# Layer 0 opens with image 0 in SBUF, evacuations on ScalarE, three eighths of v's first convolution on TensorE

## What is computed

```python
z   = group_norm(x)                       # 32 groups of 6 channels, per image
qkv = einsum('bchw,oc->bohw', z, w_qkv) + b_qkv
qkv = depthwise_conv3x3(qkv, w_dw) + b_dw # padding 1, 576 channels
q, k, v = split(qkv)                      # 4 heads of 48 channels, 4096 positions
q, k = l2norm(q), l2norm(k)
attn = softmax(q^T k * temperature)       # 4096 x 4096 per head
out  = einsum('oc,bchw->bohw', w_proj, attn v) + b_proj
x    = x + out
```

## Time and profile before

| what | value |
|---|---|
| median of 3 runs | 3560.64 us (3558.88 to 3561.38) |
| the profiled execution's own time | 3561.09 us |
| its span | 3559.3 us |
| TensorE (PE) busy | 3188.6 us, 90% |
| VectorE (DVE) busy | 1988.1 us, 56% |
| ScalarE (ACT) busy | 2096.1 us, 59% |
| GpSimd (POOL) busy | 1019.1 us, 29% |

### The profile page before, as it was taken

How to read it: one execution, slowest core, us unless ns; L and a number is a source line. 1 busy time by engine, 2 the same in 40 slices (tenths; PEclk the granted TensorE clock), 3 DMA queues, 4 the chain that set the end, 5 groups by cost and what they waited for, 6 DMA issues and landing times. The chain is left out here.

```text
span 3559.3 us, 48038 instructions
## 1 busy us (share of the span) xinstructions
PE 3188.6 (90%) x16424; PEld 1279.7 (36%) x16424; DVE 1988.1 (56%) x2522; ACT 2096.1 (59%) x2306; POOL 1019.1 (29%) x510
## 2 busy tenths in 40 slices
PE   1239999999999999999999966899999858999998
PEld 0012232222322323223222222455555424555555
DVE  4655243752257432563420145688888555888886
ACT  0015655556556565564666612688888415888886
POOL 1210202102021020020200003366566432666565
PEclk9669999999999999999999988999999979999999
DMA  6131212212103111131110033477777724877777
GB/s 179 45 77 28 60 42 45 57 45 55 50 24 77 44 37 50 35 78 32 25 44 7 10 90 92 102 139 146 145 143 139 159 75 99 145 138 144 145 144 132
DMA packets 691175, 295.71 MB, mean 83 GB/s; under 512 B 603314, under 2 KB 645042, under 8 KB 689266
## 3 DMA queue, kind: packets, MB, share of 16 engines
q1 hardware_dynamic: 690996, 293.45, 38.7%
HBM read 95.46 MB, written 34.28 MB: 36 GB/s over the span
## 5 line engine op out<-in xcount | busy, mean ns | idle before, releaser
L440 ACT ACTIVATE prob<-ps_s,cur 128x1024 f32<-128x1024 f32 x1024 | 1084.5, 1110 | 738.4 <-PE ps_s L514 736.8
L527 PE MATMUL ps_a<-prob,vt 128*64 128x512 f32 x4096 | 997.2, 608 | 0.0
L1132 POOL TENSOR_TENSOR p_lo<-gp,p_hi 128x1024 f16<-128x1024 f32 x256 | 551.9, 2166 | 402.9 <-ACT p_hi L1231 397.8
L1359 PE MATMUL ps_s<-kst,qs 128*128 128x512 f16 x2560 | 639.2, 383 | 20.3 <-DMA qs<-q_scratch 12.1
L1372 PE MATMUL ps_o<-v_hl,at_hi 128*128 128x384 f16 x2048 | 546.8, 328 | 28.4 <-DMA at_lo<-p_lo 26.9
L508 PE MATMUL ps_s<-q_a,k_a 128*128 128x512 f16 x2048 | 535.1, 383 | 7.6 <-issue 2.6
L1372 PE MATMUL ps_o<-v_hl,at_lo 128*128 128x192 f16 x2048 | 504.6, 247 | 0.0
L1606 DVE TENSOR_SCALAR_CACHE_REDUCE neg<-ps_s,mix 128x1024 f32<-128x1024 f32 x256 | 327.2, 1278 | 131.7 <-PE ps_s L1359 130.4
L527 PEld LDWEIGHTS ps_a<-prob,vt 128*64 128x64 f32 x4096 | 249.4, 136 | 412.4 <-issue 410.3
L1359 PEld LDWEIGHTS ps_s<-kst,qs 128*128 128x128 f16 x2560 | 244.8, 99 | 247.0 <-issue 23.3
L508 PEld LDWEIGHTS ps_s<-q_a,k_a 128*128 128x128 f16 x2048 | 138.0, 97 | 517.1 <-ACT prob L440 437.2
(11 more groups left out here) (176 smaller groups left out, 2763.2 us busy)
## 6 DMA issues: line engine op xcount, KB each, us to landing
z<-z_scratch SPq DMA_DIRECT2D x96, 384.0 KB, 3.9
sq<-rn_scratch SPq DMA_DIRECT2D x16, 768.0 KB, 10.6
qs<-q_scratch SPq DMA_DIRECT2D x64, 128.0 KB, 2.8
gn_x<-in_x SPq DMA_DIRECT2D x4, 1536.0 KB, 18.7
z_scratch<-gn_x SPq DMA_DIRECT2D x4, 1536.0 KB, 11.6
q_a<-hi SPq DMA_DIRECT2D x64, 96.0 KB, 2.4
rden<-den_scratch SPq DMA_DIRECT2D x64, 96.0 KB, 2.2
o_scratch<-o_s SPq DMA_DIRECT2D x64, 96.0 KB, 1.9
```

Source lines behind the costliest of these rows:

```text
L440: act.activation(prob[:, a % PR, :], ps_s[:, a % 2, :], ACT.Exp, bias=cur[:, slot:slot + 1], scale=1.0 / SPLIT).then_inc(exped, 1)
L527: ins = pe.matmul(ps_a[h * HALF:(h + 1) * HALF, j % 2, :], vt[:, slot, m, :], prob[:, a % PR, h * CH:(h + 1) * CH], start=(m == 0), stop=( ...
L1132: pool.tensor_tensor(p_lo[:, cols], prob[s][:, cols], p_hi[:, cols], ALU.subtract).then_inc(lo_made[c], 1)
L1359: ins = pe.matmul(ps_s[:, c % 2, h * CH:(h + 1) * CH], qs[:, s, qt, :], kst[:, ktile, cols], start=(t == 0), stop=(t == len(terms) - 1))
```

## The change

The block for the group norm is gone. In the new opening of layer 0:

- **Image 0 stays in SBUF.** It is loaded in four pieces of 96 x 2048, its statistics taken on VectorE (16 `bn_stats`, two more small links for a shift), and normalized there: channels 0 to 95 on VectorE, 96 to 191 on ScalarE, two halves of the pixels each. The first two projections read it in place (`project_first`); the store to `z_scratch` happens beside that.
- **Image 1's norm goes to ScalarE and GpSimd**, between other work: two copies and two squares of 96 x 4096 with an accumulated sum, two group sums on TensorE, five small GpSimd operations, two normalizing activations of 96 x 4096, all in ScalarE's program order.
- **Evacuations, squares, sums and `hi` of the first head go to ScalarE; `lo` of the first head to VectorE.** ScalarE's order holds image 1's normalization between v's third and fourth evacuated chunk.
- **The first convolutions run half by half** (`conv_half`): each tap waits for the tap before it. v's can start when five chunks are in `pad`.
- **Three eighths of v's first convolution** (chunks 5, 6, 7 of eight) become 27 products on TensorE with diagonal matrices `diag`, which ScalarE makes from `ident`; ScalarE evacuates them (`evac_far`). VectorE's second half shrinks to the 512 pixels of chunk 4.
- **The norm's root** of the first head comes from ScalarE's Sqrt and VectorE's reciprocal in place of GpSimd's power. The norm's factors come back in four pieces, each with its own semaphore. `load_z` of slot 2 now stands behind `split_out` in SP's order, followed by a wait for the last `evac_far`.
- **In the main loop** one thing changes: `split` forms u with one instruction of 112 rows in place of two of 48.

```diff
+                for c in range(4):
+                    cols = slice(c * NB, (c + 1) * NB)
+                    for h in range(2):
+                        sp.dma_start(sq[h * HALF:h * HALF + HD, cols],
+                                     rn_dram[h:h + 1, cols].partition_broadcast(HD)).then_inc(rn_first[c], 16)
+                sp.wait_ge(z_out, 16 * 2 * CT + 16 * CT)
+                sp.wait_ge(help_full, 18)
                 split_out(0, 0, None)
+                load_z(range(4), 2, 0, None)
+                sp.wait_ge(far_out, 8 - FAR)
...
             def _(act):
+                act.wait_ge(gn_op, 10)
+                for h in range(2):
+                    cols = slice(h * N // 2, (h + 1) * N // 2)
+                    act.activation(xin[:, 1, cols], xin[:, 1, cols], ACT.Identity,
+                                   bias=shift[:, 1:2], scale=gy[:, 1:2]).then_inc(z_high, 1)
+                for c in range(8):
+                    evac_project(0, c, 0)
+                for tap in range(TAPS):
+                    act.activation(diag[:, tap, :], ident[0:KR, 0:KR], ACT.Copy,
+                                   scale=vec[0:KR, 1, 1 + tap:2 + tap]).then_inc(diag_set, 1)
+                for t in range(CT):
+                    act.activation(vv[0:CP, :], xin[:, CT + t, :], ACT.Copy,
+                                   accum_out=total1[:, t:t + 1]).then_inc(gn1_op, 1)
...
+                for t in range(CT):
+                    act.activation(vv[0:CP, :], xin[:, CT + t, :], ACT.Square, bias=away1[:, t:t + 1],
+                                   accum_out=total1[:, t:t + 1]).then_inc(gn1_op, 1)
...
+                square(0)
+                square(1)
+                evac_sums(0)
+                for c in range(3):
+                    evac_project(1, c, 9)
+                act.wait_ge(gn1_pow, 5)
...
+                for t in range(CT):
+                    act.activation(xin[:, CT + t, :], xin[:, CT + t, :], ACT.Identity,
+                                   bias=shift1[:, t:t + 1], scale=gy1[:, t:t + 1]).then_inc(z1_made, 1)
+                evac_project(1, 3, CONV_OPS)
+                square(2)
+                evac_project(1, 4, CONV_OPS)
+                square(3)
+                evac_sums(1)
+                for c in range(5, 8):
+                    evac_project(1, c, CONV_OPS)
+                act.wait_ge(norm_asked, 1)
+                act.activation(nry[:, :, :], nrm[:, :, :], ACT.Sqrt).then_inc(powed, 1)
+                evac_far(5)
+                high(0)
+                high(1)
+                evac_far(6)
+                high(2)
+                high(3)
+                evac_far(7)
                 head(0, 0)
...
             def _(pe):
+                for c in range(FAR, 8):
+                    at = c - FAR
+                    for tap in range(TAPS):
+                        dy, dx = tap // 3, tap % 3
+                        ins = pe.matmul(ps_s[0:KR, at // 2, at % 2 * CH:(at % 2 + 1) * CH], diag[:, tap, :],
+                                        pad[:, c * ROWS + dy:(c + 1) * ROWS + dy, dx:dx + WW],
+                                        start=(tap == 0), stop=(tap == TAPS - 1))
+                    ins.then_inc(far_full, 1)
...
             def _(dve):
-                        for h in range(2):
-                            r = slice(h * HALF, h * HALF + HD)
-                            ins = dve.tensor_tensor(u[r, :], qk[r, cols], sq[r, cols], ALU.mult)
-                        ins.then_inc(unit_op, 1)
+                        dve.tensor_tensor(u[:, :], qk[:, cols], sq[:, cols], ALU.mult).then_inc(unit_op, 1)
...
+                conv_half(0, qk, 0, 0, 5)
+                conv_half(0, qk, 0, 1, 8)
+                conv_half(1, vv, 1, 0, 14, range(5))
                 norms_ask(0)
+                conv_half(1, vv, 1, 0, 14, range(5, 6))
+                dve.wait_ge(powed, 1)
+                dve.reciprocal(nry[:, :, :], nry[:, :, :]).then_inc(rooted_n, 1)
+                dve.wait_ge(rooted_n, 1)
                 norms(0)
+                conv_half(1, vv, 1, 0, 14, range(6, TAPS))
+                unit(0)
+                conv_half(1, vv, 1, 1, 18, range(1), ROWS)
+                for c in range(4):
+                    low(c)
+                    if c < 3:
+                        unit(c + 1)
+                    conv_half(1, vv, 1, 1, 18, range(1 + 2 * c, 3 + 2 * c), ROWS)
```

More of the change, by code:

```diff
@@ L47 @@
 USE_PAIR = USE_EVEN + USE_ODD
[L50 to L141, removed]
@@ L245, in layer0 @@
         rooted = sem("rooted")
+        x_in = [[sem(f"x_in{i}_{h}") for h in range(2)] for i in range(NT)]
+        group_in = sem("group_in")
+        gn_op = sem("gn_op")
+        gn_asked = sem("gn_asked")
+        gn_full = sem("gn_full")
+        gn_pow_asked = sem("gn_pow_asked")
+        gn_powed = sem("gn_powed")
+        z_low = sem("z_low")
+        z_high = sem("z_high")
+        gn1_op = sem("gn1_op")
+        gn1_pow = sem("gn1_pow")
+        z1_made = sem("z1_made")
+        z_out = sem("z_out")
+        rn_first = [sem(f"rn_first{c}") for c in range(4)]
+        rooted_n = sem("rooted_n")
+        diag_set = sem("diag_set")
+        far_full = sem("far_full")
+        far_out = sem("far_out")
         STEPS = NBL * KT
+        FAR = 5
         NCONST = 3
@@ new lines, in _ @@
+                act.wait_ge(gn1_op, 8)
+                for t in range(CT):
+                    act.activation(xin[:, CT + t, :], xin[:, CT + t, :], ACT.Identity,
[7 more added lines that the diff above has]
+                    evac_project(1, c, CONV_OPS)
@@ L451, in _, with project_first @@
             def _(pe):
+                def project_first(slot, c, use):
+                    n, bank = use
+                    helper_free(n)
+                    pe.wait_ge(z_low, 1 + c // 4)
+                    pe.wait_ge(z_high, 1 + c // 4)
+                    for t in range(CT):
+                        ins = pe.matmul(ps_h[0:KR, bank, :], w[:, slot, t, 0:KR], xin[:, t, c * CH:(c + 1) * CH],
+                                        start=(t == 0), stop=(t == CT - 1))
+                    ins.then_inc(help_full, 1)
                 def project(slot, tile, c, use):
@@ L454, in project @@
                     helper_free(n)
[L455 removed]
+                    pe.wait_ge(z_in[c % ZS], 16 * (2 * (tile - 2) + c // ZS + 1))
                     for t in range(CT):
@@ L485, in _ @@
                 uses = Uses(0)
+                pe.wait_ge(group_in, 16)
+                for k, src in enumerate((mean, var)):
+                    pe.wait_ge(gn_asked, k + 1)
+                    pe.matmul(ps_a[0:CP, 0, 8 * k:8 * k + CT], group[:, :], src[:, :], start=True, stop=True).then_inc(gn_full, 1)
                 pe.wait_ge(const_in, 16 * NCONST)
@@ L720, in _, with conv_half @@
-                for c in range(8):
-                    evac_project(0, c, uses.next())
-                conv(0, qk, 0, 8)
-                for q in range(2):
-                    evac_sums(q, uses.next())
-                dve.wait_ge(w_in[1], 48)
-                for c in range(8):
-                    evac_project(1, c, uses.next())
+                dve.wait_ge(vstep, 6)
+                def conv_half(slot, dst, tiles, h, n_free, taps=range(TAPS), rows=HH // 2):
+                    dve.wait_ge(help_free, n_free)
+                    for tap in taps:
+                        dy, dx = tap // 3, tap % 3
+                        r0 = h * (HH // 2)
+                        src = pad[:, r0 + dy:r0 + dy + rows, dx:dx + WW]
+                        out = dst[:, h * N // 2:h * N // 2 + rows * WW].rearrange("p (r c) -> p r c", c=WW)
+                        if tap == 0:
+                            ins = dve.tensor_scalar(out, src, vec[0:KR, slot, 1:2], vec[0:KR, slot, 10:11],
+                                                    ALU.mult, ALU.add)
+                        else:
+                            dve.wait_ge(conv_op, CONV_OPS * tiles + TAPS * h + tap)
+                            ins = dve.scalar_tensor_tensor(out=out, in0=src, scalar=vec[0:KR, slot, 1 + tap:2 + tap],
+                                                           in1=out, op0=ALU.mult, op1=ALU.add)
+                        ins.then_inc(conv_op, 1)
```

209 lines of the change are left out of this document (173 added, 36 removed).

## The result

The changed kernel takes 3454.06 us (median, 3453.19 to 3457.51), the kernel before 3559.76 us beside it; the ratio is 0.9706, 95% interval 0.9689 to 0.9723. Forecast were 3462, 3450 to 3482. The profiled execution took 3457.5 us, span 3455.7.

The account below looks back on a forecast made before the run. TensorE bounds the head loop; the 236.39 us opening was serial, its new split bound by SP. The profiled 3561.1 less 83.1 for the opening and 15.8 for the loop gave 3462.2, about 3462; range 3450 to 3482.

Parts of the forecast that it names:

- To the first product: Opening, load to first projection: image 0 in at 17.3, mean copied at 20.55, table load 1.28; first product at 28.4.
- ScalarE's list: Opening, ScalarE's ordered work from 45.8: diagonals, image 1's passes, squares, evacuations, normalization until 88.7; v's chunk 4 at 91.0.
- VectorE's new wait: Opening, ahead of v's convolution: VectorE, free at 81.6, waits for chunk 4 until 91.0, behind image 1's normalization; 9.4 us.
- The Sqrt: Opening, norm's root: ready at 105.3 after chunks 5 to 7 and a table load, against VectorE's clamp at 104.5.
- The split: Opening's last stage: SP's DMA issues set the pace, four chunks at 8.75 us, 35.0; first score at 153.3.
- What lies beside: Opening, beside the split: diagonal products 23 us until 127, transposes by 150, slot 2's z by about 160; all covered.
- The loop: Layer 0's main loop: one 112-row instruction removes three transpose waits, 8.1, and lost clock, taken 7.7; together 15.8 us.
- A: Only the opening pays; the loop's waits are replaced by others or its clock falls anyway: 3478; chance 0.12.
- B: Opening: ScalarE becomes its bound, six big passes cost 0.6 more each, extra table loads 1.3 each: 3468; chance 0.10.
- C: Opening: TensorE's clock stays low through the diagonal products, 46 us; 3 to 6 us lost, 3467; chance 0.10.
- D: Opening: diagonal products reading strided `pad` run far below projection's rate, 4.9 us each; kernel slower than before; chance 0.02.
- E: Opening: another stall of 20 to 60 us, from image 1's store or late z: 3482 to 3520; chance 0.06.

## Why the prediction was right, point by point

The direction, both gains and the bound of the opening were right; the time was 8 us too high, and the terms show where. In the profiled execution the sum gave 3462.2 and 3457.5 were measured: the opening 7.4 less, the loop 1.3 less, layer 1 4.0 more.

- **To the first product, 28.4; measured 25.61.** Two terms were too high by as much: the mean was copied 1.3 us earlier (19.25), because the last piece of image 0 was in at 16.1 and not at 17.3, and the table load of 1.28 that I had put on the path stood at 0.82, before any wait.
- **Projection, 12.3 to the fifth evacuation; measured 11.5** (25.61 to 37.14). ScalarE's 0.69 was hidden as said. TensorE reached its full rate a little sooner: the second evacuation ended 6.4 us behind the first product, before the change 7.1.
- **Taps 2.385 each; measured 19.07/8 = 2.384.** Convolution of q and k 40.9 expected, 40.8 measured.
- **ScalarE's list, 45.2 from the last evacuation to chunk 4 of v; measured 41.8** (42.29 to 84.06). This is the term that was most mis-sized. Three chunks of v took 8.0 (66.07 to 74.07) in place of 10.2, for the clock rose among them: the window at 69 to 77 us below has 0.90. The rest is small change, most of it in the passes: 3.61 and 3.71 each, 3.8 taken.
- **VectorE's new wait, 9.4; measured 6.04**, at the place named, with the releaser named. The difference is that of ScalarE's list; the convolution took what I had said.
- **"GpSimd's five small operations are long done" was wrong**, without cost by luck: they ran from 61.51 to 73.33 and ScalarE asked at 74.07.
- **The Sqrt, 0.8 of waiting; measured none.** hi of chunk 0 at 108.4 in place of 116.8.
- **The split, 35.0; measured 35.9** (108.53 to 144.44), landing 1.45. The text ahead of the result speaks of 18 DMAs for a chunk (ten from `lo`) and 72 in all. By the code they are 14 (six from `lo`) and 56, 0.64 us each, so "dearer than 0.49 each" was no sign of anything. The term was taken from the row for a whole chunk, so the sum stands.
- **What lies beside.** The products took 23.43 (23 expected), v was ready well before the split, and z of slot 2, issued from 144.48, was in time: TensorE's first product with it stands 13.8 us behind the first score without a wait.
- **The loop, 15.8; measured 17.1**, with the three waits gone, and 13.8 and 15.2 in the two runs that moved this edit alone (1826.6 - 1812.8; 1824.85 - 1809.65). Part of the 17.1 may be luck: in the nine traces of changed kernels with the loop's edit and without the still stands the loop took 1809.0 to 1813.2 us.
- **Rivals.** A fell with the loop's edit undone; VectorE's waits for GpSimd's `lo` stayed (27.0 us in the loop) and took nothing back. B did not come: passes cost less than taken. C did not come, as the windows show (last columns: granted clock, DMA share, GB/s); the first score of the run with doubled products lay within its price. D: 23.43/54 = 0.434 us a record, the same as the contiguous operand's 0.43. E did not come.

Windows of the changed kernel:

```profile
69.00:77.00 8.00, 7.77 (x17) 2.82 (x15) 7.89 (x4) 4.97 (x6) 4.24 (x2) 0.90 0.00 0
...
95.00:119.00 24.00, 23.43 (x54) 9.41 (x54) 20.23 (x22) 5.37 (x8) 0.00 (x0) 1.00 0.42 100
119.00:139.00 20.00, 5.58 (x32) 4.80 (x32) 9.37 (x15) 2.38 (x3) 0.00 (x0) 0.66 0.33 86
```

So the opening's 7.4 us are 2.8 up to the first product, 0.8 in the projection, 3.4 in VectorE's wait and 1.5 from there to the first hi, less 1.0 that the split took more. The 4.0 us of layer 1, for which the sum had nothing, brought the profiled execution nearer to it than the median is.

What I had not drawn from my own numbers: the products had no path to shorten. The same text said that a chunk's issues take 8.75 us, and a chunk's work for VectorE with all the rows would have been 7.2. Three eighths of a convolution moved to TensorE gained nothing in this opening, because SP sets the pace of the split.

## What to carry to other kernels

When an opening is serial, list for each engine and for the DMA queue what a stage costs by itself: the largest list is the bound after the change, and here it was the queue that only issues. Work taken off an engine that feeds a slower one gains nothing until that one is relieved; test it by leaving the edit out. And follow a small edit to where the busy engine waits in order: 1.2 us a chunk was worth 14 to 15 us of loop, of which 8.1 were TensorE's waits; the rest I put down to the low clock behind them.

## What the runs showed of the hardware

- **Table load without a drain.** The Sqrt's activation starts 0.02 us after its 1.28 us load (95.16 to 96.46), with an evacuation ended just before. The drain of 1380 ns that the Trainium skill (ScalarE: Activation LUTs, What ACT_TABLE_LOAD costs) adds does not show in this trace; the measurement decides.
- **GpSimd beside VectorE.** The same power on 96 x 2 took 0.71 us with VectorE idle and 2.77 beside its convolution; the multiplications took 1.8 to 2.3. By groups, us and mean ns, 15 to 80 us:

```profile
L408 POOL TENSOR_TENSOR gn_y<-gn_var,gn_half 96x2 f32<-96x2 f32 x1 | 2.8, 2767 | 33.3 <-ACT gn_var L502 33.3
...
L402 POOL TENSOR_TENSOR gn_y<-gn_var,gn_half 96x2 f32<-96x2 f32 x1 | 0.7, 709 | 14.7 <-DVE gn_var L836 14.7
```

  The Trainium skill (GPSIMD Engine Reference, Key points) says that the two share their SBUF interfaces and contend when a VectorE instruction has two SBUF inputs. A tap has two, so the trace agrees, by this one pair of instructions; no run moved one of them.
- **A still stand of ScalarE.** With 12 activations fewer ahead of the loop ScalarE stood still some 2.2 us longer (3.88 and 3.65 in place of 1.55) where two of its iterations ended; with 12 semaphore increments put in their place it did not. One trace of each; the cause is open.
- **More rows cost nothing.** A VectorE multiplication of 1024 f32 took 1217 ns on 48 rows and 1219 ns on 112.
- **One tap behind the other.** A tap on 112 x 2048 that waits for the one before took 2.384 us from start to start; with two halves alternating it was 2.27.
- **DMA issues on two queues.** Six issues of ScalarE took 3.8 us (111.87 to 115.69), 0.64 each, while SP made eight beside it in 5.4 us (109.34 to 114.70), 0.67 each.
